# The second edge pipeline of a four-layer graph network with TensorE, VectorE and ScalarE in another order

## The reference, cut to what matters

```python
# layer 3
y = segment_sum(h[src] * Wij, dst)
out = shifted_softplus(y @ W_o1 + b_o1) @ W_o2 + b_o2
x = layernorm(x + out)
# layer 4: twice  mean(x[src] over dst) @ Wl.T + bl + x @ Wr.T
h = relu(sage(x, W1l, b1l, W1r))
out = sage(h, W2l, b2l, W2r)
x = layernorm(x + out)
```

## Time and profile before

| | us |
|---|---|
| runs | 2402.45, 2410.17, 2412.42 |
| median | 2410.17 |
| profiled execution, first to last instruction (span) | 2409.0 |
| second edge pipeline in it, first `turn` to the first transfer of the next phase | 1710.4 to 2068.1 |
| its last instruction on DVE, last indirect write on POOL | 2052.2, 2062.1 |

### The profile page before, as it was taken

The page is one execution under the profiler, slowest core; times in us unless marked ns, Lnnn a source line. Parts: engine busy times, 40 slices in busy tenths (PEclk is TensorE's granted clock), DMA queues, the critical chain, the costliest instruction groups (busy, mean ns, idle before and its releaser), DMA issues. The chain is left out here.

```text
span 2409.0 us, 45629 instructions
## 1 busy us (share of the span) xinstructions
PE 2090.2 (87%) x14016; PEld 1742.8 (72%) x14016; DVE 1990.3 (83%) x2945; ACT 1791.3 (74%) x3691; POOL 1507.2 (63%) x1114
## 2 busy tenths in 40 slices
PE   5999999999997899998997888888599998487564
PEld 4999999999997677775775777776466666365464
DVE  7999999999997566666996899999488888398554
ACT  4889889988896577776775788888599998276221
POOL 6888766777730434431554655777488884688787
PEclk9999999999999899998999899999899999699776
DMA  4666666555665888886885688888377775786653
GB/s 110 146 168 156 156 167 170 162 147 162 183 183 169 222 254 252 257 238 183 201 203 134 139 185 182 203 199 194 96 188 191 192 193 152 160 204 160 170 161 104
DMA packets 322547, 427.40 MB, mean 177 GB/s; under 512 B 113683, under 2 KB 169589, under 8 KB 322308
## 3 DMA queue, kind: packets, MB, share of 16 engines
q1 hardware_dynamic: 210004, 367.20, 53.6%
q0 software_dynamic: 112000, 56.93, 13.9%
q10 hardware_dynamic: 304, 0.36, 0.0%
HBM read 239.24 MB, written 185.90 MB: 176 GB/s over the span
## 5 line engine op out<-in xcount | busy, mean ns | idle before, releaser
L1782 POOL DMA_INDIRECT acc<-combined,first_ x100 | 206.9, 2069 | 186.5 <-DMA acc<-combined,first_ 77.7
L510 PE MATMUL banks<-mats,g_hT 128*125 128x256 f32 x1000 | 260.1, 383 | 0.0
L529 PE MATMUL banks<-mats,g_zT 128*125 128x128 f32 x2000 | 238.8, 273 | 0.0
L529 PEld LDWEIGHTS banks<-mats,g_zT 128*125 128x125 f32 x2000 | 228.1, 188 | 0.0
L844 POOL DMA_INDIRECT gin_xs<-x,from_ x100 | 126.5, 1265 | 162.5 <-DMA x_of_src<-gin_xs 138.5
L510 PEld LDWEIGHTS banks<-mats,g_hT 128*125 128x125 f32 x1000 | 190.2, 190 | 27.6 <-issue 0.4
L1012 DVE TENSOR_TENSOR gin_acc<-gin_acc,gin_qr 125x512 f32<-125x512 f32 x125 | 86.6, 693 | 117.1 <-ACT gin_qr L974 86.3
L590 ACT ACTIVATE g_zT<-banks,cols 128x500 f32<-128x500 f32 x250 | 178.9, 775 | 4.8 <-PE banks L518 4.8
L573 ACT ACTIVATE g_sq<-banks 125x512 f32<-125x512 f32 x250 | 144.6, 590 | 45.1 <-PE banks L510 32.2
L437 POOL DMA_INDIRECT g_xd<-in_x,idx x100 | 124.8, 1248 | 75.3 <-PE banks L544 48.4
L1837 POOL DMA_INDIRECT em_h<-h,from_ x100 | 142.4, 1424 | 43.6 <-issue 25.6
(11 more groups left out here) (408 smaller groups left out, 6613.3 us busy)
## 6 DMA issues: line engine op xcount, KB each, us to landing
acc<-g_zero SPq DMA_DIRECT2D x126, 224.0 KB
x<-g_x SPq DMA_DIRECT2D x125, 224.0 KB
g_x<-in_xT SPq DMA_DIRECT2D x100, 250.0 KB
gin_x<-x SPq DMA_DIRECT2D x50, 448.0 KB
h<-gin_hr SPq DMA_DIRECT2D x50, 448.0 KB
al_h<-h SPq DMA_DIRECT2D x38, 448.0 KB
al_x<-x SPq DMA_DIRECT2D x38, 448.0 KB
out<-al_out SPq DMA_DIRECT2D x38, 448.0 KB
```

The lines of the kernel that those rows point to most:

```text
L510: m = nc.tensor.matmul(bank[0:P, 256 * j:256 * j + 256], HT[q % 2][:, c:c + P], K.W1c, start=False, stop=j == 1)
L529: m = nc.tensor.matmul(pO[q % 2][0:P, D * j:D * j + D], ZT[q % 2][:, h, P * j:P * j + P], K.W2[:, h, :], start=False, stop=j == R - 1 and ...
L1782: pool.indirect_dma_start(out=K.acc, out_offset=bass.IndirectOffsetOnAxis(ap=K.first[:, g, r:r + 1], axis=0), in_=CR[:, g, r * D:r * D + D ...
```

## The change: three lists in another order

No instruction is added, removed or altered, and no wait of a stage is altered either: the same stages with the same semaphores and buffers stand in other places of the lists of PE, ACT and DVE. POOL's and SP's lists are as before.

```diff
@@ TensorE
-                steps(EG, [(0, turn), (0, turn_y), (0, turn_back), (1, turn_x3), (0, first), (0, turn_yd), (1, hidden), (1, turn_x3d),
-                           (0, first_d), (1, back_h), (1, second), (0, update), (1, hidden_d), (0, update_d), (1, back_hd)])
+                steps(EG, [(1, update_d), (0, turn), (2, back_hd), (0, turn_y), (0, turn_back), (1, turn_x3), (0, first),
+                           (0, turn_yd), (1, hidden), (1, turn_x3d), (0, first_d), (1, back_h), (1, second), (0, update), (1, hidden_d)])
@@ ScalarE
-                           (0, lambda k: na.square(act, k, flat(A[k % 2]), a)), (0, size), (0, copy_yd), (0, expo), (1, relu_h), (0, log),
-                           (0, size_d), (0, na.log_of(act)), (0, lambda k: na.exp(act, k, x2)), (1, copy_x3d), (0, expo_d), (0, log_d),
-                           (1, rows_h), (1, lambda k: nc_.square(act, k, pC[0:P, :], cs)),
-                           (0, lambda k: nb.square(act, k, flat(B[k % 3]), b)), (1, relu_hd), (0, nb.log_of(act)),
-                           (0, lambda k: nb.exp(act, k, x3)), (1, nc_.log_of(act))])
+                           (0, lambda k: na.square(act, k, flat(A[k % 2]), a)), (0, size), (0, copy_yd), (1, relu_h), (0, expo),
+                           (0, na.log_of(act)), (0, log), (0, size_d), (0, lambda k: na.exp(act, k, x2)), (1, copy_x3d), (0, expo_d),
+                           (0, log_d), (1, lambda k: nc_.square(act, k, pC[0:P, :], cs)),
+                           (0, lambda k: nb.square(act, k, flat(B[k % 3]), b)), (1, rows_h), (1, relu_hd), (0, nb.log_of(act)),
+                           (1, nc_.log_of(act)), (0, lambda k: nb.exp(act, k, x3))])
@@ VectorE
-                steps(EG, [(1, apply_b), (1, nbd.reduce_of(dve)), (0, residual), (1, apply_bd), (1, sums), (0, positive), (1, average),
-                           (2, apply_c), (0, na.reduce_of(dve)), (0, soft), (0, positive_d), (0, apply_a), (0, join),
-                           (0, soft_d), (1, nc_.reduce_of(dve)), (0, nb.reduce_of(dve)), (0, join_d), (1, rows_hd)])
+                steps(EG, [(1, apply_b), (2, rows_hd), (1, nbd.reduce_of(dve)), (2, apply_c), (0, residual), (1, apply_bd),
+                           (0, na.reduce_of(dve)), (0, positive), (1, sums), (1, average), (0, soft), (0, apply_a), (0, positive_d),
+                           (0, join), (0, soft_d), (1, nc_.reduce_of(dve)), (0, nb.reduce_of(dve)), (0, join_d)])
```

More of the change, by code:

```diff
@@ L2109, in _ @@
                 nc.scalar.preload_act_table_set("natural_log_exp_and_others")
-                steps(EG, [(0, relu_b), (1, lambda k: nbd.square(act, k, flat(BD[k % 3]), bd)), (2, lambda k: nc_.exp(act, k, done)), (0, copy_y),
-                           (1, nbd.log_of(act)), (1, lambda k: nbd.exp(act, k, x3d)), (1, copy_x3),
-                           (0, lambda k: na.square(act, k, flat(A[k % 2]), a)), (0, size), (0, copy_yd), (0, expo), (1, relu_h), (0, log),
-                           (0, size_d), (0, na.log_of(act)), (0, lambda k: na.exp(act, k, x2)), (1, copy_x3d), (0, expo_d), (0, log_d),
-                           (1, rows_h), (1, lambda k: nc_.square(act, k, pC[0:P, :], cs)),
-                           (0, lambda k: nb.square(act, k, flat(B[k % 3]), b)), (1, relu_hd), (0, nb.log_of(act)),
-                           (0, lambda k: nb.exp(act, k, x3)), (1, nc_.log_of(act))])
+                steps(EG, [(0, relu_b), (1, lambda k: nbd.square(act, k, flat(BD[k % 3]), bd)), (2, lambda k: nc_.exp(act, k, done)),
+                           (0, copy_y), (1, nbd.log_of(act)), (1, lambda k: nbd.exp(act, k, x3d)), (1, copy_x3),
+                           (0, lambda k: na.square(act, k, flat(A[k % 2]), a)), (0, size), (0, copy_yd), (1, relu_h), (0, expo),
[3 more added lines that the diff above has]
+                           (1, nc_.log_of(act)), (0, lambda k: nb.exp(act, k, x3))])
             @block.vector
```

## The result

The kernel after takes 2391.52 us, median of 12 runs (2382.31 to 2399.36). The kernel before, run with it on the same chip, takes 2404.38 (12 runs, 2399.53 to 2412.99, the three shown above among them), some 6 us less than the median of those three. The ratio is 0.9946, 95% interval 0.9932 to 0.9960: 13.0 us faster, 9.6 to 16.3 by the interval. Predicted were 2395 us and 15.2 us.

The account below looks back on a forecast made before the run. A closed chain of waits through PE, ACT and DVE, 13.16 us an iteration, was taken as the bound; 13.0 + 3.2 - 1 = 15.2 us off 2409.0 gave a 2393.8 span, 2395 us as median, range 2387 to 2406.

Parts of the forecast that it names:

- PE swap: On PE, `back_hd` moves behind `turn`, into the wait for `relu_b`; claimed gain 0.43 us an iteration.
- `positive` behind `na.reduce`: On DVE, `positive` and then `first_d` follow the shorter reduce instead of the scan; claimed gain 0.12 us an iteration.
- Zero-cost edits: Other moves on DVE and ACT, among them scan, `average`, `soft`, `apply_a`, `rows_h`, `rows_hd`: claimed cost zero, `soft` having the thinnest cover.
- End of the phase: Phase end moves by 13.0 us from 23.7 iterations plus 3.2 in the drain, 16.2 in all, if POOL keeps up.
- The 13.4: Phase-end gain in us claimed if `apply_c` of group 24 became what releases the last put.
- POOL, -1: POOL's indirect transfers, held by two-operand DVE instructions, fall behind 0.5 to 0.9 us a group; 1 us taken off the gain.
- two cases: POOL's lag either settles into a fixed pattern or grows, equally likely; POOL ends 0 to 5 us late, 1 taken.
- if POOL keeps up: Condition on the 16.2 us by which the phase's end was to move: POOL's transfers hold the new pace.
- The sum: Whole kernel: 13.0 + 3.2 - 1 = 15.2 us off the profiled execution.
- rival 1: Only the PE swap pays, `na.square` coming late on ACT or `soft` eating the rest: 2399 to 2402 us; chance 0.14.
- rival 2: POOL becomes the bound, transfers let go by the scan being held again: 2416 us, past 2450 if deep; chance 0.12.
- rival 3: Nothing moves because another closed chain, perhaps over two engines, stands close behind: 2405 to 2410 us; chance 0.10.

Follow-up runs that it names:

- e1: The kernel before with only PE's new order; ACT's and DVE's orders stay old: ratio 0.9952, period 12.72 us, phase 347.82 us.
- e2: The kernel before with only DVE's and ACT's new orders, PE's order old: ratio 0.9997, period 13.06 us, phase 353.65 us.
- e9: The kernel before with PE's new order and, on DVE, only `na.reduce` and `positive` moved ahead of the scan and `average`: period 13.88 us, phase 374.15 us.
- e3: The kernel before with PE's and ACT's new orders, DVE's order old: ratio 1.0042, period 13.56 us, phase 369.55 us.
- e5: The kernel before with PE's and DVE's new orders, ACT's order old: period 12.62 us, phase 344.77 us, one run.
- e10: The kernel after with one DVE pair put back, `positive_d` ahead of `apply_a`: period 12.63 us, phase 344.26 us, one run.
- e7: The kernel after with all three orders written anew, stages spread over four iterations: ratio to before 0.9882, period 12.14 us, phase 332.01 us.
- e6: The kernel after with two groups instead of four gathered in the phase before: ratio to before 0.9903, period 12.62 us, phase 346.21 us.
- e8: The kernel after with both the deeper orders and only two groups gathered ahead: 2363.8 us, ratio to before 0.9836, period 12.14 us.
- e4: The kernel after with POOL writing only two of each group's four blocks of final rows: period 12.62 us, phase 338.39 us, one run.

## Why the prediction was right, step by step

- **PE swap, 0.43.** Right: 0.44 alone (e1), and the wait of PE halved as worked out.
- **`positive` behind `na.reduce`, 0.12.** The size is right (0.10 in e2), the closed chain too. The reason was incomplete: it rests on `apply_c` having moved (e9), for a bank that the prediction did not look at.
- **Zero-cost edits.** Right, for `soft` as long as DVE's list is the new one: with the old one its cover breaks and costs more than the change gains (e3). ACT's list was rightly priced at nothing in the period (e5).
- **End of the phase, 13.0 + 3.2.** From the first `turn` to `apply_c` of group 23 it was 335.60 us and is 319.58: 16.0 of 16.2, of it 12.8 up to the last `turn` and 3.2 in the drain, at a granted clock of 0.98 before and 0.99 after. The 13.4 for the case that `apply_c` of group 24 released the last put does not follow: with that `apply_c` 13.0 earlier and the put 0.93 behind it, its own rows give 16.3, so this case could not have decided.
- **POOL, -1.** The mis-sized term: 16.0 at `apply_c` 23 had become 14.2 by the next phase, so it is -1.8. The lag grew by 0.75 a group, within the 0.5 to 0.9; of the two cases between which I put the 1, growing came true. Of the 1.8, 1.4 is the later start of the put of group 23 and 0.5 the longer way from it to the last put. e10 shows that one pair of instructions decides the lag, and also that a POOL without it would have given back only 0.8 to 1.3: "if POOL keeps up" left out that the new order puts the scan where a punctual put begins, which then holds it for 0.75.
- **The sum** was 15.2; the phase gave 14.2 and the runs 13.0, whose interval takes in both. That 2395 came within 3.5 of the median is partly luck: the three runs that it starts from lay 5.8 above the median of the twelve, and the gain was put 2.2 too high, which partly cancel.

The rivals fell: DVE waits only 0.19 for `na.square` (rival 1), the lag stays below the 28 us from which POOL would take the whole gain (rival 2; its mechanism, a transfer let go by the scan and held again at its next start, is what after shows, at 12.62 + 0.75 = 13.4 a group in place of 14.4), and the next closed chain or bound lies lower, at 12.14 or less (rival 3, e7).

## What to carry to other kernels

Where no engine is full and the starts of one iteration add up to the period, write the closed chain down: a stage that stands in it and fits into a wait of the same chain is worth its whole duration (0.43 worked out, 0.44 measured). Before moving an instruction forward, look up whose bank the instructions that it passes were to empty; an order that gains or costs nothing in one set costs in another (e3, e9). Then look for what lies ahead of the barrier (e6) and for orders in which the next group's chain begins before this one's ends (e7): on top of the change these two gave twice as much again (e8).

## What was not expected of the hardware

A transfer on POOL that begins 0.08 us or more inside a DVE instruction with two operands in SBUF, and not in its last 0.1, ends 1.0 to 1.1 us behind it, in every kernel here, so a swap of two neighbours on DVE turned a stable lag of 1.67 into one of 15. And the clock in the drain was not the same from kernel to kernel: over the last 26 us 0.99 in after and e4 and 0.98 in e2, but 0.93 in e5, e6 and e10, after equal pauses of TensorE. No row shows what decides it. It moved the end of the last `apply_c` by 1.2 us, which reaches the phase where the last put is released by that `apply_c`, as in e5.
